# The third product of an experts' block as two products of 64 slots, one in each half of TensorE's columns

## The chip, the cores and the metric

The kernel runs on one core of one Trainium2 chip. The metric is the device time of one execution in microseconds (us), lower is better. TensorE (PE) does the matrix products, VectorE (DVE) and ScalarE (ACT) the elementwise work and the copies out of PSUM, GpSimd (POOL) the gathers and part of the elementwise work, and SyncE (SP) issues most of the transfers. PE has a second row in the profile, PEld, for the loads of the stationary operand.

## The reference, cut to what matters

A cross attention of 1024 tokens (8 x 128, width 512, 32 heads of 128) comes first; its result is added to `x`. The second part is a mixture of experts over the same 1024 tokens, 16 experts with a hidden width of 128, two experts for each token, and one shared expert:

```python
g = scores.reshape(T, GROUPS, E // GROUPS)          # 16 experts in 4 groups
_, gidx = jax.lax.top_k(g.max(axis=-1), LIM)        # 2 groups kept
_, idx = jax.lax.top_k(masked, K)                   # 2 experts for each token
def step(y, p):
    w1, b1, w2, b2, w3, b3, ge = p
    h = jax.nn.silu(xt @ w1 + b1) * (xt @ w2 + b2)
    return (y + ge[:, None] * (h @ w3 + b3), None)
```

All of it is in float32. The product `h @ w3` of the experts (128 hidden values to 512 outputs) is what the change is about.

## The kernel before, in words

The program is one pass over four stages: products of the attention's weights (to about 480 us of the span), attention over 32 heads and its output product (to about 800 us), router and shared expert (to about 853 us), and the experts' blocks (from 854 us to the end).

**The experts' blocks.** The 2048 pairs of token and expert are sorted by expert and laid into slots; each expert's slots are rounded up to whole blocks of 128. The program always runs NB = 31 blocks, since that is the most there can be; with fewer in use, the last ones belong to no token. `owner[b]` is the expert of block b. It is known only while the program runs, so the engines read it into a register (`owner_of`) and address the expert's weights by it: `ew12_s[:, e, c]` for the first two products, `w3_s[:, e]` for the third. All experts' weights lie in SBUF.

For block b, with k = b % 2 as the buffer:

- POOL gathers 128 rows of `x_rows` into `xb` (line 780), up to 11 blocks ahead (`XB`).
- PE turns `xb` into `ps_turn[k]` with four transposes (`turn_x`, line 1259); ACT copies it to `xbT[k]` (line 1583, seen under the helper's line 1319).
- PE multiplies by the first two weights at once, 256 columns, in four chunks of 128 (`block_h`, line 1275), into `ps_attn[k]`.
- DVE adds the bias (line 2113), ACT takes the silu (line 1603), DVE multiplies the two halves (line 2117) into `h_gate_b[k]`.
- PE turns that into `ps_score[k]` (`turn_h`, line 1267), and DVE copies it to `hT_b[k]` (`take_hT`, line 2103).
- PE multiplies `hT_b[k]` (stationary, 128 x 128) with `w3_s[:, e]` (moving, 512 columns) into `ps_job[k]` (`block_y`, line 1284).
- ACT scales the rows by their gates into `y_out[k]` (`take_y`, line 1590), and SP stores them to `y_slots` in DRAM (line 673). `take_y(b)` waits until the store of block b - 2 has landed.

The order on PE is written out in one loop (lines 1292 to 1309): two chunks of `block_h(b)`, `turn_h(b - 1)`, the other two chunks, `turn_x(b + 2)`, `block_y(b - 1)`. So a block's last product comes one turn of the loop after its first. On DVE a turn of the loop is `take_hT(b - 1)`, the bias of block b, the product with the silu of block b (lines 2108 to 2118). On ACT it is the silu, the copy of `xbT` two blocks on, and `take_y(b - 1)`.

**The end.** POOL waits until the blocks that hold tokens have been stored, then issues 16 gathers (line 805), which add the slots' rows to `acc`. ACT, after `take_y(30)`, issues eight stores of `acc` to the output (line 1614), each of which waits for its two gathers. Both wait for nothing else.

The loads of the experts' third weights into `w3_s` (line 668) count up `ew3_in`; PE waits for all four of them ahead of its first `block_y` (line 1307). `b3_raw` and `b3_s` (lines 287 and 288) hold the biases of the third products; they are last read by the shared expert's products (line 1224).

Of the kernel before, what the change touches and what calls it, by code (L numbers as in the profile page):

```python
# [23 lines left out]
F32 = mybir.dt.float32  # L24
# [7 lines left out]
P = 128  # L32
B = 8
D = 512
# [94 lines left out]
def build(nc, x, ctxT, mask, gains, pbias, lnw, wa, wv, wo, sw12, sw3, ew12, eb12, ew3, rw, rb, b3, out):  # L129
    with ExitStack() as stack:  # L130
# [4 lines left out]
        def place(name, shape, dtype, at=None):  # L135

            size = 1
            for n in shape[1:]:
                size *= n
            size = (size * (1 if dtype == U8 else 4) + 31) // 32 * 32  # L140
            if at is None:
                at, top[0] = top[0], top[0] + size
            return nc.alloc_sbuf_tensor_at(name, shape, dtype, offset=base + at)
# [142 lines left out]
        at_b3 = at_attn + (2 * SH + 2) * T * 4  # L286
# [8 lines left out]
        w3_s = place("w3_s", [P, E, D], F32, at_xT)  # L295
# [11 lines left out]
        def several(name, cols, count=2):  # L307
            at, cursor[0] = cursor[0], cursor[0] + count * cols * 4
            return [place(f"{name}{n}", [P, cols], F32, at + n * cols * 4) for n in range(count)]
# [4 lines left out]
        h_b, silu_b, h_gate_b, hT_b = (several("h_b", 2 * P), several("silu_b", P), several("h_gate_b", P),  # L314
                                       several("hT_b", P))
# [9 lines left out]
        assert (XB - XB_FIRST) * DX <= 2 * SH * T  # L325

        bias_all = place("bias_all", [P, E, 2 * P], F32, at_v)

        cursor = [at_wo]

# [47 lines left out]
        def bank(name):  # L378
            return stack.enter_context(nc.psum_tensor(name, [P, D], F32))

        ps_job = [bank("ps_job0"), bank("ps_job1")]
# [22 lines left out]
        def sem(name):  # L404
            return stack.enter_context(nc.semaphore(name))
# [11 lines left out]
        ew12_in, ew3_in = sem("ew12_in"), sem("ew3_in")  # L417
# [46 lines left out]
        xbT_psum, xbT_sbuf, hb_psum, hb_biased, silu_b_done, hb_gated, hbT_psum, hbT_sbuf, yb_psum, yb_sbuf = map(  # L464
            sem, ("xbT_psum", "xbT_sbuf", "hb_psum", "hb_biased", "silu_b_done", "hb_gated", "hbT_psum",
                  "hbT_sbuf", "yb_psum", "yb_sbuf"))
# [352 lines left out]
        def _(pe):  # L819
# [351 lines left out]
            def turn_logits(half):  # L1171
                pe.wait_ge(logits_copied, half + 1)
                for t in range(BH * half, BH * (half + 1)):
# [18 lines left out]
                             start=True, stop=False)  # L1192
            nc.tensor.matmul(ps_score[1][:, 0:B * E], ones[:], cum[:, 0:B].rearrange("p t e -> p (t e)"),
                             start=False, stop=True)
            nc.tensor.matmul(ps_score[1][:, B * E:(B + 1) * E], ones[:], cum[:, B],
                             start=True, stop=True).then_inc(rank_psum, 1)
# [72 lines left out]
            def owner_of(b):  # L1269
                return pe.value_load(owner[0:1, b:b + 1], min_val=0, max_val=E - 1)  # L1270
# [8 lines left out]
            def block_y(b, e):  # L1279
                k = b % 2  # L1280
                pe.wait_ge(hbT_sbuf, b + 1)
                if b >= 2:
                    pe.wait_ge(yb_sbuf, b - 1)
                nc.tensor.matmul(ps_job[k][:], hT_b[k][:], w3_s[:, e], start=True, stop=True).then_inc(yb_psum, 1)  # L1284

            pe.wait_ge(owner_ready, 1)
            pe.wait_ge(ew12_in, 16 * 4)
# [3 lines left out]
            owners = [owner_of(0)]  # L1291
            for b in range(NB):
                pe.wait_ge(xbT_sbuf, b + 1)
                if b >= 2:
                    pe.wait_ge(hb_biased, b - 1)
                if b == 0:
                    block_h(b, owners[b], range(C)).then_inc(hb_psum, 1)
                else:
                    block_h(b, owners[b], range(2))
                    turn_h(b - 1)  # L1300
                    block_h(b, owners[b], range(2, C)).then_inc(hb_psum, 1)
                if b + 1 < NB:
                    owners.append(owner_of(b + 1))
                if b + 2 < NB:
                    turn_x(b + 2)
                if b == 1:
                    pe.wait_ge(ew3_in, 16 * 4)
                if b >= 1:
                    block_y(b - 1, owners[b - 1])
            turn_h(NB - 1)  # L1310
            block_y(NB - 1, owners[NB - 1])

# [304 lines left out]
        def _(dve):  # L1618
            V = nc.vector
# [477 lines left out]
            def owner_of(b):  # L2097
                return dve.value_load(owner[0:1, b:b + 1], min_val=0, max_val=E - 1)

            def take_hT(b):  # L2100
                k = b % 2
                dve.wait_ge(hbT_psum, b + 1)
                V.tensor_copy(hT_b[k][:], ps_score[k][:, 0:P]).then_inc(hbT_sbuf, 1)

# [2 lines left out]
            owners = [owner_of(0)]  # L2107
            for b in range(NB):
                k = b % 2
                if b >= 1:  # L2110
                    take_hT(b - 1)
                dve.wait_ge(hb_psum, b + 1)
                V.tensor_tensor(h_b[k][:], ps_attn[k][:, 0:2 * P], bias_all[:, owners[b]], ALU.add).then_inc(hb_biased, 1)
                if b + 1 < NB:
                    owners.append(owner_of(b + 1))
                dve.wait_ge(silu_b_done, b + 1)
                V.tensor_tensor(h_gate_b[k][:], silu_b[k][:], h_b[k][:, P:2 * P], ALU.mult).then_inc(hb_gated, 1)
            take_hT(NB - 1)

# [57 lines left out]
```

## Time and profile before

| | |
|---|---|
| device time, median of 2 runs | 967.07 us (966.99 to 967.15) |
| the profiled execution | 969.12 us, its span 967.4 us |
| around the span | 1.7 us |
| PE busy | 941.0 us, 97% of the span |
| PEld, DVE, ACT, POOL busy | 785.6, 638.9, 410.9, 277.1 us |
| granted clock of PE, mean over the span | 0.996 |

The span is the time from the first to the last instruction of the profiled execution. Matmuls are pipelined and their ends are modelled, so the busy time of a line on PE counts overlaps; the chain of waits gives each piece its own share of time.
### The profile page before, as it was taken

What the parts mean: (1) busy time and instruction counts of PE and PEld (TensorE: products, weight loads), DVE (VectorE), ACT (ScalarE), POOL (GpSimd) and SP (SyncE); (2) the same over time, 40 slices, a digit from 0 to 9 for tenths busy, and PEclk for the clock granted to TensorE, in tenths of its full rate; (3) what the DMA queues carried; (4) which work ended last, traced back from release to release, by engine and by line L of the source; (5) the groups of instructions that cost most, each with busy time, mean ns of one, the idle gap of its engine ahead of it and who ended that gap; (6) DMA issues with size and microseconds to landing.
All of it is one profiled execution on the core that took longest, in us unless ns stands there. A gap on an engine that the chain in (4) does not pass through costs nothing.

```text
span 967.4 us, 13972 instructions
## 1 busy us (share of the span) xinstructions
PE 941.0 (97%) x4843; PEld 785.6 (81%) x4843; DVE 638.9 (66%) x1069; ACT 410.9 (42%) x1004; POOL 277.1 (29%) x251
## 2 busy tenths in 40 slices
PE   7999999999999999999999999999999999889994
PEld 6888888888888788888888989889898887667772
DVE  6877669666665865544777878778787777743331
ACT  6336554333333432214555464464544435224442
POOL 1252434433433033003122121121222011143364
PEclk9999999999999999999999999999999999999998
DMA  7655454645456635639747645637456059555589
GB/s 267 218 197 185 180 199 154 220 174 215 178 203 211 220 148 183 219 135 322 266 167 272 233 144 210 232 131 259 143 198 210 1 223 347 189 181 171 173 184 252
DMA packets 86788, 193.76 MB, mean 200 GB/s; under 512 B 8608, under 2 KB 29344, under 8 KB 85312
## 3 DMA queue, kind: packets, MB, share of 16 engines
q1 hardware_dynamic: 79312, 177.67, 51.5%
q0 software_dynamic: 4784, 12.58, 5.7%
q10 hardware_dynamic: 2624, 2.62, 0.8%
q8 instruction: 40, 0.66, 0.3%
q14 instruction: 28, 0.23, 0.1%
HBM read 121.74 MB, written 71.11 MB: 199 GB/s over the span
## 4 chain that ended last, share of the span: by engine, by line
PE 74%; DVE 4%; DMA 2%; issue 2%; ACT 1%; POOL 0%; ACTq 0%; SPq 0%; DVEq 0%
PE ps_job L824 7%; PE ps_job L826 7%; PE ps_job L825 7%; PE ps_attn L1040 6%; PE ps_score L1012 6%; PE ps_attn L1275 5%; PE ps_turn L1026 3%; PE ps_job L1284 2%; PE ps_score L884 1%; PE ps_score L885 1%; PE ps_attn L884 1%; PE ps_attn L885 1%; PE ps_attn L886 1%; PE ps_score L886 1%; PE ps_turn L1259 1%
## 5 line engine op out<-in xcount | busy, mean ns | idle before, releaser
L748 POOL TENSOR_TENSOR score_bias<-mask_bias,pos_bias 128x1024 f32<-128x1024 f32 x32 | 78.0, 2439 | 293.3 <-DVE probs L1842 185.6
L1329 ACT ACTIVATE probs<-probs,neg_max 128x128 f32<-128x128 f32 x256 | 99.5, 392 | 95.6 <-DVE neg_max L1845 95.6
L709 POOL TENSOR_TENSOR w_sum<-w_raw 128x256 f32<-128x256 f32 x30 | 23.6, 787 | 179.3 <-PE ps_score L886 77.1
L1040 PE MATMUL ps_attn<-pT,v_s 128*128 128x128 f32 x512 | 62.7, 276 | 1.7 <-issue 1.4
L1275 PE MATMUL ps_attn<-ew_s,xbT 128*128 x248 | 62.3, 380 | 1.0 <-ACT xbT L1319 1.0
L1012 PE MATMUL ps_score<-kq_s 128*128 128x128 f32 x512 | 62.4, 275 | 0.0
L1040 PEld LDWEIGHTS ps_attn<-pT,v_s 128*128 128x128 f32 x512 | 59.8, 192 | 2.4 <-issue 1.6
L1275 PEld LDWEIGHTS ps_attn<-ew_s,xbT 128*128 128x128 f32 x248 | 44.6, 190 | 20.3 <-issue 15.1
L1012 PEld LDWEIGHTS ps_score<-kq_s 128*128 128x128 f32 x512 | 59.8, 192 | 0.2
L1869 DVE TENSOR_TENSOR acc<-ps_job,acc 128x512 f32<-128x512 f32 x56 | 37.9, 685 | 29.6 <-PE ps_job L826 29.6
L780 POOL DMA_INDIRECT xb<-x_rows,token_of x31 | 31.2, 1007 | 86.2 <-ACT y_out L1590 41.3
L1319 ACT ACTIVATE w_hi<-w_sum 128x1024 fp32r<-128x1024 f32 x30 | 31.8, 1061 | 52.8 <-POOL w_sum L714 52.8
L1319 ACT ACTIVATE w_hi<-w_raw 128x768 fp32r<-128x768 f32 (+3 forms) x38 | 31.2, 822 | 53.7 <-PE ps_score L886 26.5
L1319 ACT ACTIVATE pT<-ps_turn 128x512 f32<-128x512 f32 x64 | 34.5, 592 | 45.6 <-PE ps_turn L1026 45.6
L1842 DVE TENSOR_TENSOR probs<-ps_score,score_bias 128x512 f32<-128x512 f32 x64 | 43.7, 682 | 15.2 <-PE ps_score L1012 12.6
L824 PE MATMUL ps_job<-wo_hi,attn_even_lo 128*128 128x512 f32 x128 | 51.2, 400 | 0.0
L1681 DVE TENSOR_TENSOR w_lo<-w_raw,w_hi 128x768 fp32r<-128x768 f32 (+1 forms) x31 | 40.7, 1313 | 14.2 <-ACT w_hi L1319 13.9
L826 PE MATMUL ps_job<-wo_hi,attn_even_hi 128*128 128x512 f32 x128 | 50.0, 391 | 0.0
L825 PE MATMUL ps_job<-wo_lo,attn_even_hi 128*128 128x512 f32 x128 | 49.8, 389 | 0.0
L1329 ACT ACTIVATION_READ_ACCUMULATOR probs<-probs,neg_max 128x1 f32 x256 | 48.8, 190 | 0.0
L1856 DVE TENSOR_TENSOR probs<-probs,row_scale 128x512 f32<-128x512 f32 x64 | 44.3, 692 | 2.2
L1845 DVE TENSOR_REDUCE neg_max<-probs 128x4 f32<-128x512 f32 x64 | 43.9, 686 | 2.2
(465 smaller groups left out, 2585.0 us busy)
## 6 DMA issues: line engine op xcount, KB each, us to landing
kq<-st SPq DMA_DIRECT2D x32, 1024.0 KB, 4.2
kq_s<-kq SPq DMA_DIRECT2D x64, 512.0 KB, 4.5
v_s<-v_all SPq DMA_DIRECT2D x8, 2048.0 KB, 10.8
w_raw<-wa_dram SPq DMA_DIRECT2D x31, 512.0 KB, 5.6
v_all<-st SPq DMA_DIRECT2D x24, 512.0 KB, 3.7
y_slots<-ones SPq DMA_DIRECT2D x32, 256.0 KB, 4.7
wo_raw<-wo_dram SPq DMA_DIRECT2D x8, 1024.0 KB, 6.9
ew_s<-ew_dram SPq DMA_DIRECT2D x4, 2048.0 KB, 13.2
```

Source lines behind the costliest of these rows:

```text
L748: nc.gpsimd.tensor_tensor(score_bias[:], mask_bias[:], pos_bias[:, i % 2].unsqueeze(1).broadcast_to([P, B, P]), ALU.add).then_inc(bias_rea ...
L824: nc.tensor.matmul(psum, l_lo, r_hi, start=(k == 0), stop=False)
L825: nc.tensor.matmul(psum, l_hi, r_lo, start=False, stop=False)
L826: last = nc.tensor.matmul(psum, l_hi, r_hi, start=False, stop=(closed and k == n - 1))
L1012: last = nc.tensor.matmul(ps_score[half][:, cols(b)], kq_s[:, i % 2, 1, tok], kq_s[:, i % 2, 0, tok], start=True, stop=True)
L1040: last = nc.tensor.matmul(ps_attn[half][:, cols(b)], v_s[g % 2][:, BH * half + b, cols(j)], pT[:, half, cols(b)], start=True, stop=True)
L1275: last = nc.tensor.matmul(ps_attn[k][:, 0:2 * P], xbT[k][:, cols(c)], ew12_s[:, e, c], start=(c == 0), stop=(c == C - 1))
L1319: return nc.scalar.activation(dst, src, ACT.Copy)
L1329: last = nc.scalar.activation(probs[i % 2][:, half, b], probs[i % 2][:, half, b], ACT.Exp, bias=neg_max[:, i % 2, half, b:b + 1], accum_ou ...
L1842: V.tensor_tensor(probs[i % 2][:, half], ps_score[half][:].rearrange("p (b k) -> p b k", b=BH), score_bias[:, BH * half:BH * (half + 1)], ...
L1845: V.tensor_reduce(neg_max[:, i % 2, half], probs[i % 2][:, half], AX.X, ALU.max, negate=True)\
L1856: V.tensor_tensor(probs[i % 2][:, half], probs[i % 2][:, half], row_scale[:, half].unsqueeze(2).broadcast_to([P, BH, P]), ALU.mult).then_i ...
```

## The change

The 128 slots of a block are split: the first 64 columns of `hT_b[k]` are the stationary operand of one product, whose result goes to partitions 0 to 63 of `ps_job[k]`; the other 64 are that of a second product, whose result goes to partitions 64 to 127 of the same bank. Both have all 128 rows (hidden values) and 512 moving columns. The first still reads `w3_s[:, e]` by the register; the second reads `w3_b[k]`, a copy at a fixed address. DVE makes the copy in `take_hT(b)`, ahead of its wait for the transpose. For block 0 it waits for the loads of the third weights; from block 2 on it waits until the product of block b - 2, which read the same buffer, is done. The two buffers take the places of `b3_raw` and `b3_s`.

```diff
+        w3_b = [place(f"w3_b{n}", [P, D], F32, at_b3 + n * D * 4) for n in range(2)]
...
                 pe.wait_ge(hbT_sbuf, b + 1)
                 if b >= 2:
                     pe.wait_ge(yb_sbuf, b - 1)
-                nc.tensor.matmul(ps_job[k][:], hT_b[k][:], w3_s[:, e], start=True, stop=True).then_inc(yb_psum, 1)
+
+                nc.tensor.matmul(ps_job[k][0:P // 2, :], hT_b[k][:, 0:P // 2], w3_s[:, e], start=True, stop=True)
+                nc.tensor.matmul(ps_job[k][P // 2:P, :], hT_b[k][:, P // 2:P], w3_b[k][:], start=True, stop=True)\
+                  .then_inc(yb_psum, 1)
...
             def take_hT(b):
+
                 k = b % 2
+                if b == 0:
+                    dve.wait_ge(ew3_in, 16 * 4)
+                if b >= 2:
+                    dve.wait_ge(yb_psum, b - 1)
+                V.tensor_copy(w3_b[k][:], w3_s[:, owners[b]])
                 dve.wait_ge(hbT_psum, b + 1)
                 V.tensor_copy(hT_b[k][:], ps_score[k][:, 0:P]).then_inc(hbT_sbuf, 1)
```

## Rows read from the trace of the kernel before

**Rows 1.** The page: busy time of the engines over the span.

```profile
PE 941.0 (97%) x4843; PEld 785.6 (81%) x4843; DVE 638.9 (66%) x1069; ACT 410.9 (42%) x1004; POOL 277.1 (29%) x251
```

**Rows 2.** Busy time by stretch: start:end, length, five engines, PEclk, DMA share, GB/s.

```profile
850.00:855.00 5.00, 4.05 (x22) 3.22 (x22) 2.61 (x4) 1.08 (x2) 1.15 (x2) 1.00 0.03 11
...
854.60:937.00 82.40, 80.24 (x384) 60.01 (x385) 25.21 (x75) 36.34 (x74) 35.01 (x33) 1.00 0.60 176
937.00:957.60 20.60, 18.22 (x76) 11.46 (x74) 6.05 (x18) 7.94 (x17) 15.95 (x11) 1.00 1.06 215
```

**Rows 3.** Chain of waits in order of time, one period of the blocks: start, length, what.

```profile
896.46 0.86 PE ps_job L1284 x2
897.32 0.86 PE ps_attn L1275 x4
898.19 0.11 PE ps_score L1267
898.30 0.86 PE ps_attn L1275 x4
899.16 0.44 PE ps_turn L1259 x4
899.60 0.86 PE ps_job L1284 x2
```

**Rows 4.** Timeline of the same period: L1284, its weight loads, and DVE.

```profile
896.19 0.30 PEld L1284 LDWEIGHTS ps_job<-w_s,hT_b 128*128 128x128 f32 x2
896.30 1.02 PE L1284 MATMUL ps_job<-w_s,hT_b 128*128 x2
...
896.97 0.29 DVE L2117 TENSOR_TENSOR h_gate_b<-silu_b,h_b 128x128 f32<-128x128 f32 x1 [0.38 <-issue]
...
898.34 0.29 DVE L2103 COPY hT_b<-ps_score 128x128 f32<-128x128 f32 x1 [1.07 <-PE ps_score L1267]
```

**Rows 5.** Chain of waits around the small transposes of the router, L1174.

```profile
814.92 0.35 PE ps_turn L1174 x4
815.26 0.43 PE ps_attn L1146
815.69 0.23 PE ps_attn L1147
```

**Rows 6.** L1174 in the timeline and by line; group of weight loads of 96 columns.

```profile
814.85 0.42 PE L1174 MATMUL ps_turn<-ident,logitsT 16*128 16x16 f32 x4
...
L1174 PE MATMUL ps_turn<-ident,logitsT x8: 208/208/232, 814.8 to 816.3; 16*128 16x16 f32 x8
...
L1203 PEld LDWEIGHTS ps_score<-ident,gates 128*96 128x96 f32 x4 | 0.5, 125 | 0.1
```

**Rows 7.** Groups of copies and casts on DVE, shapes apart.

```profile
L1818 DVE COPY st<-ps_attn 128x512 f32<-128x512 f32 x2 | 1.3, 687 | 0.4 <-PE ps_attn L852 0.4
L1972 DVE CAST b_s<-b_raw 96x512 fp32r<-96x512 f32 x1 | 0.4, 418 | 0.0
```

**Rows 8.** Timeline of DVE in the first blocks: a late copy.

```profile
864.41 0.29 DVE L2103 COPY hT_b<-ps_score 128x128 f32<-128x128 f32 x1 [3.71 <-remote]
```

**Rows 9.** Timeline of the last blocks: PE, ACT, and ACT's stores of the output.

```profile
955.35 1.12 PE L1284 MATMUL ps_job<-w_s,hT_b 128*128 x2 [0.47 <-DVE hT_b L2103]
...
957.58 0.69 ACT L1590 ACTIVATE y_out<-ps_job,xb 128x512 f32<-128x512 f32 x1 [2.48 <-DMA y_slots<-y_out]
957.61 6.27 ACTq L1614 DMA_DIRECT2D out_dram<-acc  x8
```

**Rows 10.** Scalings until 922 us; POOL's timeline; gathers with us to landing.

```profile
L1590 ACT ACTIVATE y_out<-ps_job,xb x19: 680/687/688, 862.3 to 919.4; 128x512 f32<-128x512 f32 x19
...
925.55 0.22 POOL L800 TENSOR_TENSOR slot_at<-base_i,row_i 128x16 int32<-128x16 int32 x1 [0.54 <-DMA y_slots<-y_out]
...
954.45 1.55 POOL L805 DMA_INDIRECT acc<-y_slots,slot_at  x1 [0.30 <-issue]
...
acc<-y_slots,slot_at POOLq DMA_INDIRECT x16, 6.6
```

## The prediction, made before the changed kernel ran

> **What bounds the kernel now.** I read the page first: PE is busy for 97% of the span [rows 1]. That is an average over four stages, and the change touches only the experts' blocks, so I asked for the stretches of that stage. From 854.6 to 937 us PE is busy 80.24 of 82.4 us at a granted clock of 1.00 (2.4 GHz) while DVE has 25.2, ACT 36.3 and POOL 35.0; the 16 DMA engines are at 0.60 [rows 2]. PE is what limits it. The chain in order of time then gives the price of each step of PE: 0.86 us for four matmuls of L1275, 0.11 for the turn of L1267, 0.86 for four more, 0.44 for the four turns of L1259, and 0.86 for the two matmuls of L1284, the product that is changed. A period lasts 899.60 - 896.46 = 3.14 us, and these five add up to 3.13, so there is no gap in it [rows 3]. Whatever the new product takes beyond 0.86 us is paid in every one of the 31 blocks, as long as PE sets the pace.
>
> What comes after the blocks decides if that reaches the end. Two things run there. The 19th scaling starts at 919.4, and POOL's last step ahead of the gathers, released by a store of `y_slots`, at 925.55; so 19 blocks hold tokens. The gathers are issued until 954.45 + 1.55 = 956.0; each lands some 6.6 us after its issue, so the last at about 962.6 [rows 10]. ACT's last scaling starts at 957.58, and its eight stores follow at once and take 6.27 us to issue; the span of 967.4 ends 9.8 us after the 957.58 [rows 9]. The stores follow each other directly, so I take ACT's row as the one that ends the kernel: every microsecond by which block 30 is later moves the end, while the gathers move only with 19 of the 31 blocks.
>
> **The change part by part.**
>
> *The product itself.* Before, it is two matmuls of 512 columns, 0.43 us each [rows 3]. After, it is four: the two of the first half (call them A1, A2), then the two of the second (B1, B2), each still 512 columns, because halving the stationary side takes nothing from the moving side. At best, then, nothing is won: even if both halves ran side by side from start to end they would need the 0.86 us that one full product needs. The question is only how much is lost. At the lower end A and B run wholly beside each other: 0.86. At the upper end nothing overlaps: 4 x 0.43 = 1.72. I take a value between them from the order. The four stand in the queue as A1, A2, B1, B2, and the trace shows PE's matmuls starting in the order of the program throughout. A2 needs the same half as A1 and can start only when A1 has streamed; B1 stands behind A2; so only A2 and B1 can overlap, and B2 follows B1. B1 also needs its weights. In the trace the first load of L1284 starts at 896.19 and its matmul at 896.30, 0.11 later [rows 4]; a load of 96 columns takes 0.125 us [rows 6], so for 64 I take 0.11 as well, from the start of A2 on, since each load comes just ahead of its matmul. That makes 0.43 (A1) + 0.11 + 0.43 (B1, over A2) + 0.43 (B2) = 1.40 us, 0.54 more than before.
>
> The Trainium skill, "TensorE: Matmul & The Clock Gate", Part 3 on packing small matmuls, says that matmuls in different tiles of the array run at the same time but start and end strictly in program order, and gives 2.38x for three column tiles of 32. No row here shows column tiles at all; by that rule A2 would run beside B1, and A1 not, as in the sum. The same part says that a weight load overlaps a running matmul only where the row groups differ, which both halves here share. By the rows it overlaps with equal rows: the two loads of L1284 begin at 896.19, while the turns ahead of it hold the chain until 896.46 [rows 3, 4]. If the rule did hold in the halves, four loads of 0.11 would be added to the four passes instead of the one in the sum, 31 x 0.33 = 10 us more: 1000.
>
> *Going into the halves and out of them.* The product stands between turns and products that use the whole array. The nearest rows are the router's small transposes, which use 16 rows of it: four of them take 0.35 us on the chain, and the product behind them takes 0.43, the one after that 0.23 [rows 5]. Four such transposes at their own pace would be 4 x (0.42 - 0.208) / 3 = 0.28 [rows 6]. So it costs 0.07 on the way in and 0.20 on the way out, 0.27 together. The lower bound is nothing, if column halves need no such pause; the upper I set at twice that, 0.54, since the matmuls here are longer to run out. I take 0.27, as the only row of the kind.
>
> The Trainium skill, "TensorEngine Tiling (Array Packing)", Key Properties, says that a change of tiling mode, unlike a change of tile, drains TensorE. By that rule a pause is paid twice in each of the 31 blocks, and the sum stands; the trace agrees as far as the 0.20 us behind L1174 goes. Were column halves free of it, the sum would be 31 x 0.54 - 0.54 - 0.96 = +15, 982 us.
>
> *The copy of the weights on DVE.* 128 x 512 float32 from SBUF to SBUF is not in the trace. A copy of the same shape out of PSUM takes 0.687 us, a cast of 96 x 512 within SBUF 0.418 [rows 7]; I take 0.42, the nearer. It stands between the end of L2117 (896.97 + 0.29 = 897.26) and the next L2103, in front of which DVE idles 1.07 us waiting for PE [rows 4]. Even 0.69 fits into that, and behind it the product doesn't begin before 899.60, almost a microsecond after the copy of hT has ended (898.63). So it costs nothing on the path, and less still if the period grows. Its new waits: for b >= 2 the product of block b - 2 must be done, and on PE that lies a whole turn of the loop earlier; behind the copy only L2103 and the next bias are queued. The wait of block 0 for the third weights: the DMA engines have fallen to 0.03 busy between 850 and 855 us [rows 2], so they have landed before the first block begins (854.6).
>
> *What is given back.* Two pauses get smaller. The copy of hT for block 1 comes at 864.41, after DVE has idled 3.71 us for a cause that is not PE [rows 8]; PE waits for it, and will arrive one lengthened product later, which saves that length once. And the last scaling starts at 957.58 although block 30 ends at 955.35 + 1.12 = 956.47; it could follow some 0.15 later, so 0.96 are lost to the store of block 28 [rows 9], while the DMA engines are at 1.06 [rows 2]. With the gathers done earlier relative to the blocks, this wait should go.
>
> *The sum.* Per block 0.54 + 0.27 = 0.81 us; 31 of them 25.1. Given back: 0.81 + 0.96 = 1.8. Net 23.3 us. The span becomes 967.4 + 23.3 = 990.7, and the same execution 969.12 + 23.3 = 992.4. The runs shown lie 2.05 us below that execution, so the forecast for the median is 967.07 + 23.3 = **990 us**. The gathers would end at 962.6 + 19 x 0.81 = 978, ahead of ACT's last scaling (956.6 + 25.1 - 0.8 = 980.9), so they stay off the path.
>
> **The rivals.**
>
> 1. *No overlap at all.* The two halves follow each other as two ordinary products, as every pair of matmuls in the trace does. The block then pays 0.86 + 0.27 = 1.13; 31 x 1.13 = 35.0, less 1.13 + 0.96 = 2.1: +32.9, 1000 us. For it: no two matmuls of this trace run beside each other. Against it: the halves write different partitions, use different columns, and the copy gives each its own source. With loads that don't hide (0.11 each) it would be up to 4 x 0.11 x 31 = 14 more. In this case the change doesn't do what it says, since the halves don't work together.
>
> 2. *The other side: both halves wholly beside each other.* A1 with B1 and A2 with B2. The point from which it decides: the product with its pauses has to stay under 0.86 + 0.68 = 1.54 us for the time to stay within 2% (31 x 0.68 - 0.68 - 0.96 = 19.4). With the load of B and the pauses the block pays 0.11 + 0.27 = 0.38: 11.8 - 0.4 - 1.0 = +10, 977 us. If neither is paid, the 0.96 stays as it is too and it is 967. For it: a period would hold the same number of moving columns as before, and fp32r products stream 512 columns in 0.23 us [rows 5], so PE can be fed twice as fast as one float32 pass asks. Against it: the order in which the four passes are issued.
>
> 3. *A bigger pause.* With the overlap of the forecast, but 0.54 us for the two pauses of a block: 31 x 1.08 - 1.08 - 0.96 = +31, 998 us. For it: a pass of L1284 has longer to run out than a small transpose. It can't be told by the total from rival 1, only by the rows of L1284.
>
> **How the numbers follow.** The forecast's case has a chance of 0.48, rival 1 0.28, rival 2 0.14, rival 3 0.10. Two percent of 967 is 19.3 us, about what a measurement of this kernel can tell from no change; it lies 4 us below the forecast. Pauses of 0.15 instead of 0.27 would bring the forecast's own case to 987, the edge of it, so of its 0.48 I put 0.38 above 2% and 0.10 within. Slower by over 2%: 0.38 + 0.28 + 0.10 = 0.76. Within 2%: 0.10 + 0.13 = 0.23. Faster: 0.01, since no term of the sum is negative but what is given back. The range reaches down to rival 2 (975) and up past rival 1 (1004); I leave out the loads that don't hide.
>
> **What would show each step.** L1284 would have four matmuls and four loads for a block, loads of about 0.11 us, and B1 starting some 0.1 us after A2. The period in the chain would be 3.95 us instead of 3.14; 4.27 would be rival 1, 3.5 or less rival 2. The first L1275 behind the product should come about 0.2 us later than the streaming alone explains. The copy on DVE should last 0.3 to 0.7 us and L2103 should still be released by PE. ACT's last scaling should be released by PE, not by a store. I would be wrong if the period doesn't change, if L1284 waits for DVE, or if the added time lies outside the blocks.

## The result, and the profile after

The changed kernel takes 975.41 us (975.33 to 975.49, 2 runs) against 967.07: a ratio of 1.0076, with an interval from 1.0046 to 1.0105. It is slower by 8.3 us, where 23.3 were forecast. The profiled execution has a span of 973.8 us and took 975.49. Below, times and ratios are of fast executions alone; one of 3410.96 us (the kernel before, on the second chip) and one of 2480.01 (pairs with halves) stand apart and are left out.

The period of the blocks has grown by 0.34 us, from 3.14 [rows 3] to 901.66 - 898.18 = 3.48. This is the chain of waits in order of time (start, length, what):

```profile
898.18 0.57 PE ps_job L1287
898.75 0.01 PE ps_job L1288
898.76 0.42 PE ps_job L1287
899.18 0.01 PE ps_job L1288
899.19 1.06 PE ps_attn L1277 x4
900.25 0.11 PE ps_score L1269
900.36 0.87 PE ps_attn L1277 x4
901.22 0.44 PE ps_turn L1261 x4
901.66 0.57 PE ps_job L1287
```

L1287 is the product of the first half, L1288 that of the second, L1277 the old L1275. Each of the two matmuls of a float32 product is called a pass here. The product holds 0.57 + 0.01 + 0.42 + 0.01 = 1.01 us, against 0.86 before. The pass that comes first takes 0.57 instead of 0.43, so 0.14 to 0.15 are paid on the way in. The four matmuls of L1277 behind it take 1.06 instead of 0.86, so 0.20 are paid on the way out; with 0.145 for the way in that is 0.345 us in each block. Everything else in the period is as it was. The second half's passes add 0.01 us each to the chain. The timeline shows why:

```profile
901.59 0.64 PE L1287 MATMUL ps_job<-w_s,hT_b 128*64 x1
901.59 0.13 PEld L1288 LDWEIGHTS ps_job<-w_b,hT_b 128*64 128x64 f32 x1
901.60 0.64 PE L1288 MATMUL ps_job<-w_b,hT_b 128*64 128x512 f32 x1
901.64 0.14 PEld L1287 LDWEIGHTS ps_job<-w_s,hT_b 128*64 128x64 f32 x1
...
902.07 0.59 PE L1287 MATMUL ps_job<-w_s,hT_b 128*64 x1
902.08 0.59 PE L1288 MATMUL ps_job<-w_b,hT_b 128*64 128x512 f32 x1
```

The first passes of both halves start together, at 901.59 and 901.60, and so do the second ones, at 902.07 and 902.08. The forecast had the order first, first, second, second; the trace has them alternating, and wholly beside each other. The loads take 0.13 to 0.14 us for 64 columns, and the next one of the first half (901.64) already runs beside that of the second.

The loads also show what the pauses are made of. These are the first loads of the product behind L1284 before, and behind the halves after:

```profile
896.73 0.19 PEld L1275 LDWEIGHTS ps_attn<-ew_s,xbT 128*128 128x128 f32 x1 [0.24 <-issue]
```

```profile
899.12 0.73 PEld L1277 LDWEIGHTS ps_attn<-ew_s,xbT 128*128 128x128 f32 x4 [0.81 <-issue]
```

Before, that load starts 0.59 us ahead of the end of L1284 (897.32 [rows 3]); after, it starts 0.07 ahead of the end of the halves (899.19). The load that was hidden lies bare.

On DVE the copy takes 0.42 us (group by line, and one period of its timeline), and the copy of hT behind it is still released by PE, after 1.08 us of waiting as before [rows 4]:

```profile
L2112 DVE COPY w_b<-w_s 128x512 f32 x31 | 13.2, 426 | 0.0
```

```profile
898.90 0.42 DVE L2112 COPY w_b<-w_s 128x512 f32 x1
900.39 0.29 DVE L2114 COPY hT_b<-ps_score 128x128 f32<-128x128 f32 x1 [1.08 <-PE ps_score L1269]
```

By stretch (columns as in [rows 2]), PE is idle for 0.35 us between 854.6 and 937; before it was 2.16, of which 1.81 at block 1 (see below, under what is given back):

```profile
854.60:937.00 82.40, 82.05 (x403) 52.33 (x403) 31.45 (x93) 33.74 (x70) 31.20 (x30) 1.00 0.54 162
```

At the end, ACT's last scaling is 965.25 - 957.58 = 7.67 us later, and it still waits for a store. The store in the chain, and ACT's timeline:

```profile
959.53 5.53 DMA y_slots<-y_out
```

```profile
965.25 0.69 ACT L1595 ACTIVATE y_out<-ps_job,xb 128x512 f32<-128x512 f32 x1 [2.69 <-DMA y_slots<-y_out]
965.27 5.21 ACTq L1619 DMA_DIRECT2D out_dram<-acc  x8
```

So the theory after the result: two halves of the array work wholly side by side, which gains nothing here, since each half still streams two passes of 512 columns, as the full product did; what is paid is the change from the whole array to the halves (0.15) and back (0.20), once in each block. The rivals: the copy on DVE or its waits cost part of it; or the halves share something, so that together they are slower than one alone.

### The profile page after: what moved, and what is told of

Read it like the earlier page. It is cut to its first block, busy times and chain, and to the rows that moved or that the text cites. A ratio compares the mean times of both kernels' runs of the same rounds, so it can differ in the third digit from the quotient of the medians.

```text
span 973.8 us, 14158 instructions
## 1 busy us (share of the span) xinstructions
PE 949.9 (98%) x4905; PEld 780.3 (80%) x4905; DVE 648.7 (67%) x1100; ACT 411.1 (42%) x1004; POOL 277.6 (29%) x251
## 4 chain that ended last, share of the span: by engine, by line
PE 76%; DVE 4%; DMA 1%; issue 1%; ACT 0%; POOL 0%; SPq 0%; ACTq 0%; DVEq 0%
PE ps_job L826 7%; PE ps_job L828 7%; PE ps_job L827 7%; PE ps_attn L1042 6%; PE ps_score L1014 6%; PE ps_attn L1277 6%; PE ps_job L1287 3%; PE ps_turn L1028 3%; PE ps_score L886 1%; PE ps_score L887 1%; PE ps_attn L887 1%; PE ps_attn L886 1%; PE ps_attn L888 1%; PE ps_score L888 1%; PE ps_turn L1261 1%; PE ps_attn L954 1%
## 5 line engine op out<-in xcount | busy, mean ns | idle before, releaser
L1277 PEld LDWEIGHTS ps_attn<-ew_s,xbT 128*128 128x128 f32 x248 | 42.2, 190 | 29.9 <-issue 24.7
L1277 PE MATMUL ps_attn<-ew_s,xbT 128*128 x248 | 65.2, 392 | 0.9 <-ACT xbT L1324 0.9
## 6 DMA issues: line engine op xcount, KB each, us to landing
v_s<-v_all SPq DMA_DIRECT2D x8, 2048.0 KB, 10.7
```

The costliest lines, as they stand in the source:

```text
L1277: last = nc.tensor.matmul(ps_attn[k][:, 0:2 * P], xbT[k][:, cols(c)], ew12_s[:, e, c], start=(c == 0), stop=(c == C - 1))
```

## The experiments

All times stand beside the kernel before on the same chip. Its median was 970.38, 967.43 and 969.58 us on the three chips, so ratios are compared.

**The copy without the halves.** The product as before, in the whole array; the copy and its waits stay.

```diff
-                nc.tensor.matmul(ps_job[k][0:P // 2, :], hT_b[k][:, 0:P // 2], w3_s[:, e], start=True, stop=True)
-                nc.tensor.matmul(ps_job[k][P // 2:P, :], hT_b[k][:, P // 2:P], w3_b[k][:], start=True, stop=True)\
-                  .then_inc(yb_psum, 1)
+                nc.tensor.matmul(ps_job[k][:], hT_b[k][:], w3_s[:, e], start=True, stop=True).then_inc(yb_psum, 1)
```

> The copy of the weights on VectorE with its waits, and the product as before, in the whole array. Theory 1 (the 8.3 us are the changes between the whole array and its halves, 0.15 us on the way in and 0.20 on the way out of each block, and nothing else): the copy is hidden, 966 to 968 us, period 3.14. Theory 2 (the copy, by its waits or by the port that it takes, costs part of it): 970 us or more.

Measured: 970.45 us, ratio 1.0001 (0.998 to 1.0022), period 900.10 - 896.97 = 3.13. Nothing is seen of the copy, within the 2 us of the interval. The 970 by which theory 2 was to be told is that chip's level: the kernel before had 970.38 there.

**One half left out.**

```diff
                 nc.tensor.matmul(ps_job[k][0:P // 2, :], hT_b[k][:, 0:P // 2], w3_s[:, e], start=True, stop=True)\
+                  .then_inc(yb_psum, 1)
-                nc.tensor.matmul(ps_job[k][P // 2:P, :], hT_b[k][:, P // 2:P], w3_b[k][:], start=True, stop=True)\
-                  .then_inc(yb_psum, 1)
```

> Leaves out the second half of each block's last product, so slots 64 to 127 of each block keep what the bank held. Theory 1 (the two halves run side by side from start to end, only the changes cost): leaving one out saves nothing, 974 to 976 us, period 3.48. Theory 3 (the halves share something, and together take longer than one alone): below 973, period below 3.4.

Measured: ratio 1.0074 (1.0046 to 1.0103), the same as with both halves. The chain of waits of this run has a period of 902.53 - 899.05 = 3.48 and the same two pauses:

```profile
899.05 1.00 PE ps_job L1287 x2
900.06 1.06 PE ps_attn L1277 x4
...
902.09 0.44 PE ps_turn L1261 x4
```

One half alone takes 1.00 us for its two passes, both together 1.01. The second half is free, and nothing that the two share limits them.

**Both products in the same half.**

```diff
-                nc.tensor.matmul(ps_job[k][P // 2:P, :], hT_b[k][:, P // 2:P], w3_b[k][:], start=True, stop=True)\
+                nc.tensor.matmul(ps_job[k][0:P // 2, :], hT_b[k][:, P // 2:P], w3_b[k][:], start=True, stop=True)\
```

> The second product also goes to the first half of the columns and writes over the first one's result, so the output of slots 0 to 63 is that of 64 to 127 and the others keep what the bank held. Theory 1: the four passes follow each other, so the block pays 0.86 us more than the changed kernel, period 4.34, 975.4 + 31 x 0.86 = 1002 us. The order of the records also tells who puts the passes side by side: if they come as first, first, second, second here, then the order of the passes in the changed kernel is TensorE's own doing; if they come alternately, it is the order of the program as it was lowered.

Measured: 999.09 us, ratio 1.029 (1.0256 to 1.0323), 28.7 us over the kernel before. The chain:

```profile
898.42 1.00 PE ps_job L1287 x2
899.42 0.86 PE ps_job L1288 x2
900.28 1.06 PE ps_attn L1277 x4
...
902.75 1.00 PE ps_job L1287 x2
```

The period is 902.75 - 898.42 = 4.33, 0.85 more than in the changed kernel, and now the passes come first, first, second, second. The time stays 3 us below the 1002 that were expected. That is rival 1 of the prediction as it would look; it needs only the position of the second product to be changed. The passes keep to the program's order where they need the same columns. Their loads cost nothing, though all have the same rows and columns:

```profile
898.83 0.14 PEld L1288 LDWEIGHTS ps_job<-w_b,hT_b 128*64 128x64 f32 x1 [0.29 <-issue]
```

It lies under the first pass of L1287, which streams until 898.42 + 0.57 = 898.99, and the three passes behind that one take 0.43 us each.

**A small product in a half, ahead of the full one.** The kernel before, plus the change of mode and almost no work.

```diff
+                nc.tensor.matmul(ps_job[k][0:P // 2, 0:8], hT_b[k][:, 0:P // 2], ident[:, 0:8], start=True, stop=True)
                 nc.tensor.matmul(ps_job[k][:], hT_b[k][:], w3_s[:, e], start=True, stop=True).then_inc(yb_psum, 1)
```

> The kernel before, with one more product ahead of each last product: 64 columns of hT by 8 columns of the identity, in the first half; its result is written over by the product. It has the two changes of mode and no work to speak of. Theory 1: 0.35 us of pauses and some 0.05 to 0.1 for the small product itself in each block, 31 x 0.40 to 0.45 less what is given back in the tail (2.4): 977 to 980 us. Theory 3 (the cost belongs to the large product in halves): under 971 us.

Measured: ratio 1.0074 (1.0048 to 1.0099), 7.4 us over the kernel before. In the chain of waits the product itself is whole (0.86 before) and pays for its neighbour:

```profile
899.62 0.21 PE ps_job L1284 x2
899.84 1.05 PE ps_job L1285 x2
900.89 0.86 PE ps_attn L1275 x4
...
903.17 0.21 PE ps_job L1284 x2
```

The small product (L1284) takes 0.21, of which the theory gives 0.15 to the pause, and the full one (L1285) 1.05, 0.19 more. The period is 3.55. So the pauses are there without the large product in halves; the cost belongs to the changes.

A small stationary operand alone doesn't bring the pause. The router's products in the trace of the kernel before have 16 stationary columns and one matmul each, and follow turns of the whole array:

```profile
808.91 0.44 PE ps_turn L835 x4
809.35 0.23 PE ps_score L824
```

L824 takes the 0.23 us that each of its successors takes, with no pause on the way in, and its load starts at 809.08, 0.27 ahead of the end of the turns. What sets it apart from the small float32 product no run shows.

**The changed kernel again, four quarters, and pairs of blocks.** The changed kernel was run again as the measure for the three that follow.

> The changed kernel again, on the chip on which the next ones run, so that they can be compared with it. Theory 1: the ratio to the kernel before is 1.0076 again, within its interval of 0.3%, and the period 3.48.

Measured: 975.91 us, ratio 1.0089 (1.0064 to 1.0115), period 901.35 - 897.87 = 3.48.

Four products of 32 slots, one in each quarter of the columns:

```diff
+                for n in range(4):
+                    rows = slice(n * P // 4, (n + 1) * P // 4)
+                    last = nc.tensor.matmul(ps_job[k][rows, :], hT_b[k][:, rows], w3_s[:, e] if n == 0 else w3_b[k][:],
+                                            start=True, stop=True)
+                last.then_inc(yb_psum, 1)
```

> The last product as four of 32 slots in the four quarters of the columns, the last three with the copy. Theory 1 (what lies in different columns runs side by side, the pauses are per change of mode): the period stays at 3.48 to 3.52 and the time within 2 us of the changed kernel. If products ran side by side only in pairs, the four would take 0.86 us more: period 4.3, 27 us more.

Measured: 975.05 us, ratio 1.0076 (1.0058 to 1.0094); eight passes take 0.99 us in the chain, and the period is 905.60 - 902.13 = 3.47:

```profile
902.13 0.99 PE ps_job L1289 x8
903.12 1.06 PE ps_attn L1277 x4
...
905.60 0.99 PE ps_job L1289 x8
```

Then the number of changes was halved. PE issues the last products of two blocks together at every second turn of the loop, and ACT the two scalings; once with the halves, once in the kernel before:

```diff
-                if b >= 1:
+                if b >= 2 and b % 2 == 0:
+                    block_y(b - 2, owners[b - 2])
                     block_y(b - 1, owners[b - 1])
...
-                if b >= 1:
+                if b >= 2 and b % 2 == 0:
+                    take_y(b - 2)
                     take_y(b - 1)
```

> The changed kernel with the last products of two blocks issued together at every second turn of the loop (and their scalings too), so 16 changes into the halves and back instead of 31. Theory 1: 15 x 0.345 = 5.2 us less than the changed kernel, as far as the new order itself costs nothing (the next run tells that). If the pause belonged to each product: no difference.

> The same pairing of two blocks' last products in the kernel before, in the whole array. It has no changes of mode to save, so by theory 1 it is within 1 us of the kernel before, and what it differs by is to be taken off the run with pairs in halves.

Measured: with halves 976.95 us, ratio 1.0098 (1.007 to 1.0126); in the whole array 972.43, ratio 1.0049 (1.003 to 1.0067). The second expectation failed: pairing itself costs 972.43 - 967.43 = 5.0 us in the whole array. With halves that uses up what fewer changes save, and the pairs can't be told from the unpaired 975.91. Against each other they tell what was asked: 976.95 - 972.43 = 4.5 us for 16 visits to the halves, where 16 x 0.345 = 5.5; unpaired it is 975.91 - 967.43 = 8.5 for 31. The medians of three and four runs are a weak witness here; the periods are the strong one. The period of two blocks is 903.70 - 896.84 = 6.86 with halves and 908.30 - 901.77 = 6.53 in the whole array, so 0.33 for a pair: one pause in and one out. The chain of the pairs in the whole array also shows where most of the 5.0 come from:

```profile
901.77 1.72 PE ps_job L1284 x4
...
904.35 0.11 PE ps_score L1267
...
905.77 0.86 PE ps_attn L1275 x4
...
906.65 0.33 PE ps_score L1267
906.98 0.89 PE ps_attn L1275 x4
```

Every second turn of `h_gate_b` takes 0.33 instead of 0.11, because with no last product ahead of the block's first one, DVE and ACT are only just in time: 0.22 + 0.03 in each of 15 pairs, 3.8 us. So 0.86 us of last product in every turn of the loop is also a cover for the bias, the silu and the product of the block.

**One source for both halves.**

```diff
-                nc.tensor.matmul(ps_job[k][0:P // 2, :], hT_b[k][:, 0:P // 2], w3_s[:, e], start=True, stop=True)
+                nc.tensor.matmul(ps_job[k][0:P // 2, :], hT_b[k][:, 0:P // 2], w3_b[k][:], start=True, stop=True)
```

> Both halves read the copy of the weights, so both stream the same 512 columns of SBUF. Theory 1 (nothing is shared that limits): the same as the changed kernel, 975 to 976 us, period 3.48. If two streams from one place got in each other's way (the reason one could have for a copy beyond the form of the address): a longer period.

Measured: 978.4 us against 969.58 on that chip, ratio 1.0083 (1.0052 to 1.0114), period 902.11 - 898.63 = 3.48. Two streams from one place don't disturb each other, so a copy isn't needed for speed. The chain's first pass still takes 0.57, though now neither half reads by the register, so the pause on the way in isn't a cost of the register. In no run does the second half read by the register; if the copy is needed at all isn't shown.

**The product ahead of the turns.** `block_y(b - 1)` comes before `turn_x(b + 2)`.

```diff
+                if b >= 1:
+                    block_y(b - 1, owners[b - 1])
                 if b + 2 < NB:
                     turn_x(b + 2)
...
-                if b >= 1:
-                    block_y(b - 1, owners[b - 1])
```

> The changed kernel with the last product ahead of the four turns of the block after next instead of behind them. Theory 1: one change in and one out as before; the sum of the two pauses may differ with what stands on either side, but stays between 0.25 and 0.45 us, period 3.4 to 3.6, within 3 us of the changed kernel.

Measured: ratio 1.0061 (1.0037 to 1.0086), period 902.05 - 898.62 = 3.43. In the chain:

```profile
899.20 0.42 PE ps_job L1287
899.62 0.01 PE ps_job L1288
899.62 0.59 PE ps_turn L1261 x4
900.21 0.86 PE ps_attn L1277 x4
```

The way out costs 0.15 ahead of the turns (0.59 instead of 0.44) and 0.20 ahead of a product. A load of a turn is the shorter one in the trace of before (group by line, 0.141 against 0.190 us), and the difference fits the load that the pause lays bare. All the pauses fit it: 0.13 in the chain for a first load of 0.108 (32 columns, the quarters), 0.14 to 0.15 for 0.134 (64 columns), 0.15 for 0.141 (a turn), 0.20 for 0.190 (128 columns). In each of the four the pause is the first load and some 0.01 to 0.02. That the exposed load is the cause is argued from these four and not shown by a run of its own.

**Two products in the first half, then one in the second.** This asks who sets the passes side by side.

```diff
                 nc.tensor.matmul(ps_job[k][0:P // 2, :], hT_b[k][:, 0:P // 2], w3_s[:, e], start=True, stop=True)
+                nc.tensor.matmul(ps_job[k][0:P // 2, :], hT_b[k][:, P // 2:P], w3_b[k][:], start=True, stop=True)
                 nc.tensor.matmul(ps_job[k][P // 2:P, :], hT_b[k][:, P // 2:P], w3_b[k][:], start=True, stop=True)\
```

> Three products of 64 slots for each block: first half of the columns, first half again (written over), second half. The output of slots 0 to 63 is that of 64 to 127. The first theory of the order (TensorE starts the second half's passes as soon as that half is free, past those that wait for the first half): the second half's first pass starts with the very first pass. The other (passes of neighbouring products are set alternately when the program is lowered, and TensorE keeps their order): it starts with the third pass. Either way 4 passes in line, 1.72 us and the pauses: period 4.34, 1002 us. If TensorE kept the order first, first, second for whole products: 6 passes in line less one, 2.15 us, 1015.

Measured: 1001.29 us, ratio 1.031 (1.0282 to 1.0339). In the program the order is L1287, L1288, L1289; in the timeline L1289, the product of the second half, is second:

```profile
900.69 0.64 PE L1287 MATMUL ps_job<-w_s,hT_b 128*64 x1
900.70 0.64 PE L1289 MATMUL ps_job<-w_b,hT_b 128*64 128x512 f32 x1
901.17 0.59 PE L1287 MATMUL ps_job<-w_s,hT_b 128*64 x1
901.18 0.59 PE L1289 MATMUL ps_job<-w_b,hT_b 128*64 128x512 f32 x1
901.60 1.02 PE L1288 MATMUL ps_job<-w_b,hT_b 128*64 128x512 f32 x2
```

The period is 900.76 - 896.42 = 4.34. L1289 starts 0.01 us after the very first pass, past three passes of the first half that still wait. Setting neighbours alternately could not have done this. By the rows, a half takes its next matmul without regard to what waits for the other half. An order that was set on purpose before the program ran, with L1289 moved forward, would look the same in the starts; the signal speaks against it. It keeps the order: L1289 carries it and has streamed by 901.77, but ACT's scaling starts at 902.78. By the chain of waits of this run L1288 ends at 901.77 + 0.84 = 902.61, so the scaling follows 0.17 later, about as it does behind an ordinary product (0.15):

```profile
902.78 0.69 ACT L1596 ACTIVATE y_out<-ps_job,xb 128x512 f32<-128x512 f32 x1 [1.05 <-PE ps_job L1289]
```

**The kernel before once more, for its trace.**

> The kernel before once more, on another chip, for its trace. If the late copy on VectorE at block 1 (3.7 us of idle, 1.8 us of it on TensorE) belongs to that one execution and not to the kernel, it is absent or of another size here, and the time is up to 2 us less than the 969.1 of the profiled execution. If it belongs to the kernel, it is at the same block with the same length.

Measured: 967.91 us, span 966.2. The late copy on DVE is there again, at the same block, with another length, so the expectation holds in neither form:

```profile
863.47 0.29 DVE L2103 COPY hT_b<-ps_score 128x128 f32<-128x128 f32 x1 [3.06 <-remote]
```

Ordinarily this copy starts 0.31 us after the turn on PE that it waits for; here the turn starts at 861.17, 2.30 before it. By this measure it is late at block 1 in nine of the fourteen traces: 2.95 and 2.30 us in the two of the kernel before, 2.82 with the copy alone, 2.51 with one half, 1.97 with the product first, 1.92 with one source, 1.61 with the small product, 1.06 with two then one and 0.94 with the same half. It is not late in the two of the changed kernel, with the quarters, and in the two with pairs. Six of the nine have the same instructions on DVE as the changed kernel, so the program of DVE alone doesn't decide it. What it waits for, and how often it comes in which kernel, the runs don't tell.

## Why the prediction was wrong

*The product itself: wrong, and the step that failed.* The failed step is the overlap of the four passes. The prediction let only the first half's second pass and the second half's first pass overlap ("B1 stands behind A2"), and priced the product at 1.40 us, 0.54 more. All four overlap in pairs: A1 with B1, A2 with B2. Without the pause the product takes some 0.87 us, and the term of 0.54 is 0.01. It was 31 x 0.54 = 16.7 of the 25.1 us. I had taken the order of the trace for a rule of the engine, but a trace in which no two products stand in different columns can't show anything else. Two products in one half (period 4.33) and two plus one (the third starts second) show where the order holds and where not. Rival 2 was this case, with a chance of 0.14 and 977 us; that its time came so near is in part luck, since its 0.11 for a load isn't paid and the pauses cost 0.08 more than it had. The rule of the Trainium skill that matmuls in different tiles start and end strictly in program order ("TensorE: Matmul & The Clock Gate", Part 3) does not hold for the starts here: L1289 starts at 900.70, and L1288, which stands ahead of it in the program, at 901.60. For the signal, what the rule is used for there, it holds. The other rule, that a load overlaps a matmul only where the row groups differ, doesn't hold either: in the run with both products in the same half, the load at 898.83 lies under a pass with the same rows, as loads already did in the whole array.

*The pauses: right in kind, sized too small.* Forecast 0.07 in and 0.20 out, from the router's small transposes; measured 0.15 in and 0.20 out. 31 x 0.345 = 10.7 us instead of 31 x 0.27 = 8.4. The small product in a half, one half alone, and pairs of blocks each gave the same two pauses, so they belong to the change of mode and not to the product. This agrees with the Trainium skill ("TensorEngine Tiling (Array Packing)", Key Properties), which has a change of mode drain the engine and gives no size: the load behind the halves starts only 0.07 us before they end, where it was 0.59. The 0.07 on the way in came from transposes with 16 rows, another kind of change, and was half of what column halves cost. The sentence that no row shows column tiles left out L824 with its 16 stationary columns, which shows no pause at all; going by it, the way in would have been put at nothing.

*The copy on DVE: right.* 0.42 forecast, 0.426 measured, hidden behind DVE's wait for PE; with the copy alone the ratio is 1.0001.

*What is given back: half right, by another way than forecast.* Of 31 x 0.345 = 10.7 us the last scaling shows 7.67 in the two profiled executions. The late copy on DVE accounts for 2.07: PE waited 1.81 for it, and L1284 behind the wait took 1.12 instead of 0.86. It was in the one trace and not in the other, where I had expected it in both, shortened by one lengthened product. The wait of the last scaling for the store of block 28 did not go away (2.48 us idle before, 2.69 after), since that store took 5.53 us where it had taken 4.26:

```profile
953.13 4.26 DMA y_slots<-y_out
```

The rest, 10.7 - 2.07 - 7.67 = 1.0 us, went in the last blocks, where the DMA engines are busiest and PE had gaps of its own before; which gap took how much is not told apart. ACT's eight stores took 5.21 us instead of 6.27 to issue. The difference of the spans is 6.4 us and that of the medians 8.3; the profiled execution of before stands 2.05 above its median, that of the kernel after 0.08. The late copy alone doesn't explain that: the second execution of before has it too, with 1.15 us of waiting on PE, and took 967.91, at the low end of what that chip gave (967.92 to 972.68 in ten executions). The cause of the 2.05 stays open.

*The place and the end: right.* The time went into the blocks, L1284's own rows and the product behind; ACT's row ended the kernel as said.

*The range and the chances.* The range (975 to 1004) held the time by 0.4 us, and only because it reached down to rival 2, but "slower by over 2%" had 0.76 and was wrong: 0.86 + 0.35 = 1.21 us lies under the 1.54 from which the 2% would have been passed.

## What to carry to other kernels

Splitting a product that fills the array gained nothing here, although its parts overlap wholly: before splitting, count the moving columns in line on each part of the array, 1024 here before and after. Parts in different columns are free beside each other (a second half 0.01 us, four quarters no more than two halves), so halves should pay where products with at most 64 stationary columns would otherwise queue (two in one half took 0.85 us more than one in each), and where they can be issued together, since each visit to the halves costs 0.30 to 0.35 us in float32. Before counting on an order that a trace shows, ask if anything in it could have come in another order.

## What the runs showed of the hardware that I had not expected

- Matmuls start out of the program's order across column halves: the third of three products began 0.01 us after the first and 0.90 us before the second. ACT, which waits for its signal, still started only 0.17 us after the second had ended.
- A float32 product of 64 stationary columns and 512 moving ones takes as long as one of 128 (1.00 us with the pause in, 0.86 without), alone or with a neighbour in the other half; four of 32 columns side by side take 0.99 with the pause in.
- Going into halves costs 0.15 us, coming back 0.20 ahead of a product with a load of 128 x 128 and 0.15 ahead of a transpose, each some 0.01 to 0.02 more than the load that stands first. Products of 16 stationary columns with one matmul each pay nothing on the way in.
- The late copy on DVE at block 1 (0.94 to 2.95 us behind its turn, where 0.31 is ordinary) comes in some executions and not in others of the same DVE program; both executions of the kernel before have it, and neither of the changed kernel.
